# Attention scores as pairs of 64-partition products, with the attention stage ordered by head pairs

## The reference

```
scores = jnp.einsum('bqgnh,bknh->bnqk', gq, k) / jnp.sqrt(jnp.float32(d_head))
scores = jnp.where(causal, IGNORE, scores)
pattern = jax.nn.softmax(scores, axis=-1)
z = jnp.einsum('bknh,bnqk->bqnh', v, pattern)
attn_out = jnp.einsum('bqnh,nhd->bqd', z, W_O)
```

## Time and profile before

| | |
|---|---|
| median of the runs | 610.9 us |
| span of the profiled execution | 607.1 us (its own time is not listed apart from the span) |
| PE busy | 541.2 us, 89% |
| PE weight loads | 425.8 us, 70% |
| DVE / ACT / POOL busy | 387.2 / 305.8 / 182.2 us |
| fills of queries, keys, values | 176.2 to 218.9 us |
| attention, first to last score | 220.2 to 385.85 us |
| rest of attention and routing | to 419.6 us |
| experts | the rest |

### The profile page before, as it was taken

The page is one execution under the profiler, slowest core; times in us unless marked ns, Lnnn a source line. Parts: engine busy times, 40 slices in busy tenths (PEclk is TensorE's granted clock), DMA queues, the critical chain, the costliest instruction groups (busy, mean ns, idle before and its releaser), DMA issues. The chain is left out here.

```text
span 607.1 us, 9890 instructions
## 1 busy us (share of the span) xinstructions
PE 541.2 (89%) x3178; PEld 425.8 (70%) x3179; DVE 387.2 (64%) x972; ACT 305.8 (50%) x552; POOL 182.2 (30%) x269
## 2 busy tenths in 40 slices
PE   1997976999988989999999999954899999999995
PEld 1645864797877866666766766733888888888883
DVE  4986678647375564776865757535666666666661
ACT  1486362215315574555555646413666666666661
POOL 3704449102033123464423231011122222222222
PEclk9999999899999985999999999985999999999999
DMA  8995020000010038000000000991122221222212
GB/s 337 391 335 173 2 70 1 0 1 1 0 36 1 1 123 362 9 28 28 28 1 28 1 27 8 357 354 55 17 37 31 35 37 34 33 34 34 34 18 25
DMA packets 25779, 47.44 MB, mean 78 GB/s; under 512 B 2192, under 2 KB 21136, under 8 KB 25360
## 3 DMA queue, kind: packets, MB, share of 16 engines
q1 hardware_dynamic: 21232, 41.35, 19.0%
q0 software_dynamic: 4080, 5.15, 5.7%
q10 hardware_dynamic: 432, 0.49, 0.3%
HBM read 32.01 MB, written 14.98 MB: 77 GB/s over the span
## 5 line engine op out<-in xcount | busy, mean ns | idle before, releaser
L1596 PE MATMUL ps<-split,xsT 128*128 128x352 f32 x552 | 95.9, 331 | 0.7 <-DVE split L1246 0.7
L1596 PEld LDWEIGHTS ps<-split,xsT 128*128 128x128 f32 x552 | 89.9, 192 | 1.0 <-issue 1.0
L1118 DVE TENSOR_REDUCE nmax<-ps 128x1 f32<-128x128 f32 (+7 forms) x64 | 48.3, 756 | 42.1 <-PE ps L1507 41.2
L1246 DVE TENSOR_TENSOR split<-early,split 128x1408 fp32r<-128x1408 f32 x46 | 72.6, 1618 | 1.9 <-ACT split L784 1.9
L1618 PE MATMUL ps<-mid,work 128*128 (+1 forms) x276 | 67.9, 387 | 0.8 <-ACT work L773 0.8
L784 ACT CAST split<-early 128x1408 fp32r x46 | 62.7, 1366 | 0.9 <-issue 0.9
L1618 PEld LDWEIGHTS ps<-mid,work 128*128 128x128 f32 (+1 forms) x276 | 49.7, 189 | 13.4 <-issue 8.7
L1227 DVE TENSOR_TENSOR work<-work,ps 128x704 f32<-128x704 f32 x23 | 20.4, 888 | 56.8 <-PE ps L1596 56.8
L565 POOL TENSOR_TENSOR rstd<-mhalf 128x1 f32<-128x1 f32 x23 | 11.4, 496 | 138.7 <-ACT work L780 138.7
L1502 PE MATMUL ps<-k_hi,q_split 128*128 128x512 f32 (+3 forms) x96 | 43.8, 456 | 3.2 <-ACT mid L715 1.3
L1504 PE MATMUL ps<-k_lo,q_split 64*128 64x512 f32 (+3 forms) x96 | 44.0, 458 | 0.0
(11 more groups left out here) (249 smaller groups left out, 1160.0 us busy)
## 6 DMA issues: line engine op xcount, KB each, us to landing
early<-m_w SPq DMA_DIRECT2D x16, 704.0 KB, 8.4
expert_in<-pad SPq DMA_DIRECT2D x8, 1040.0 KB, 12.5
mid<-m_w SPq DMA_DIRECT2D x8, 640.0 KB, 10.4
work<-expert_in SPq DMA_DIRECT2D x23, 130.0 KB, 2.5
early<-factors SPq DMA_DIRECT2D x1, 2048.0 KB, 12.4
early<-wq SPq DMA_DIRECT2D x1, 2048.0 KB, 16.8
mid<-f_w SPq DMA_DIRECT2D x1, 2048.0 KB, 21.2
rows<-x_in SPq DMA_DIRECT2D x2, 512.0 KB, 5.3
```

The source lines that it names most:

```text
L1118: V.tensor_reduce(nmax[:, u:u + 1], src, AX_X, ALU.max, negate=True).then_inc(s_max, 1)
L1246: V.tensor_tensor(lo, (ew1, ew3)[w][:, bass.ds(e, 1), :], hi.bitcast(F32), ALU.subtract).then_inc(s_wlo[w], 1)
L1596: last = mm(ps[:, 2 * w + a, 0:IH], xsT[px][b][:, k, :], split_w[w][pw][:, k, a * IH:(a + 1) * IH], start=(k == 0 and px == pw), stop=(k = ...
```

## The change

`k_hi` and the two query parts become 128-partition tensors of four head pairs: a head has one half of the partitions. A key fill is one copy by ScalarE and one subtraction by VectorE. GpSimd makes `q_hi` and `q_lo` by one instruction each per pair. `scores(m)` now does a pair: the two masks first, then three 64-row products per bank (high x high, low x high, high x low), head 0 in rows 0 to 63 and head 1 in rows 64 to 127 in turn. For tiles 0 to 3 a pair has two banks of four, for tiles 4 to 7 all four. The loops of PE, ACT and DVE run over pairs m, with the once-per-tile work at given m % 4. As `k_hi` is half as large, five blocks of w3 load early and three late.

```diff
--- before.py
+++ after.py
@@ -100,8 +100,8 @@
-        K_AT = 2 * E * KD * I - HEADS * T
-        k_hi = view(overlay("k_hi", K_AT, HEADS * T), 0, HEADS, T)
+        K_AT = 2 * E * KD * I - QB * T
+        k_hi = view(overlay("k_hi", K_AT, QB * T), 0, QB, T)
@@ -155,7 +155,7 @@
-        q_split = view(overlay("q_split", 5120, HEADS * P), 0, HEADS, P)
+        q_hi, q_lo = (view(overlay(name, 5120 + i * QB * P, QB * P), 0, QB, P) for i, name in enumerate(("q_hi", "q_lo")))
         work = sb("work", 7 * 1024)
@@ -312,14 +312,21 @@
+        PAIRS = HEADS // 2
+        STEPS = TT * PAIRS
+
         def k_parts(q):
-
             g, j = divmod(q, 12)
             c = slice(g * GW, (g + 1) * GW)
-            for h in range(2):
-                half, other = slice(h * DH, (h + 1) * DH), slice((1 - h) * DH, (2 - h) * DH)
-                n = 2 * (j - 4) + h
-                yield half, k_hi[half, n, c], k_hi[other, n, c], k_lo[half, j - 4, c]
+            return k_hi[:, j - 4, c], k_lo[:, j - 4, c]
+
+        def score_banks(u):
+            m, h = divmod(u, 2)
+            return 2 * h if m // PAIRS >= GT else 2 * (m % 2) + h
+
+        def score_row(u):
+            at = score_banks(u)
+            return ps[:, at:at + 2, :].rearrange("p a b -> p (a b)")[:, 0:(u // HEADS + 1) * P]
@@ -385,8 +392,8 @@
             for e in range(early_w3, E):
-                heads_over = -(-(E * KD * I + (e + 1) * KD * I - K_AT) // T)
-                sp.wait_ge(s_sc, (TT - 1) * HEADS + min(heads_over, HEADS))
+                pairs_over = -(-(E * KD * I + (e + 1) * KD * I - K_AT) // T)
+                sp.wait_ge(s_sc, (TT - 1) * HEADS + 2 * min(pairs_over, PAIRS))
                 sp.dma_start(ew3[:, e], m_w3[:, e]).then_inc(s_e13, 16)
@@ -508,22 +515,14 @@
             def split_queries(m):
-
-
-                i, pair = divmod(m, HEADS // 2)
-                if m >= HEADS // 2:
-                    pool.wait_ge(s_sc, 2 * (m - HEADS // 2) + 2)
-                for h in range(2):
-                    half, other = slice(h * DH, (h + 1) * DH), slice((1 - h) * DH, (2 - h) * DH)
-                    nc.gpsimd.tensor_copy(q_split[half, 2 * pair + h, :],
-                                          qT[half, pair, i * P:(i + 1) * P]).then_inc(s_qhi, 1)
-                pool.wait_ge(s_qhi, 2 * m + 2)
-                for h in range(2):
-                    half, other = slice(h * DH, (h + 1) * DH), slice((1 - h) * DH, (2 - h) * DH)
-                    nc.gpsimd.tensor_tensor(q_split[other, 2 * pair + h, :], qT[half, pair, i * P:(i + 1) * P],
-                                            q_split[half, 2 * pair + h, :].bitcast(F32), ALU.subtract).then_inc(s_qs, 1)
-                    pool.wait_ge(s_qs, 2 * m + h + 1)
-
+                i, pair = divmod(m, PAIRS)
+                if m >= PAIRS:
+                    pool.wait_ge(s_sc, 2 * (m - PAIRS) + 2)
+                q = qT[:, pair, i * P:(i + 1) * P]
+                nc.gpsimd.tensor_copy(q_hi[:, pair, :], q).then_inc(s_qhi, 1)
+                pool.wait_ge(s_qhi, m + 1)
+                nc.gpsimd.tensor_tensor(q_lo[:, pair, :], q, q_hi[:, pair, :].bitcast(F32),
+                                        ALU.subtract).then_inc(s_qs, 1)
@@ -705,10 +704,7 @@
                     act.wait_ge(s_qkv, q + 1)
-                    for half, hi, hi_other, lo in k_parts(q):
-                        nc.scalar.copy(hi, ps[half, 2 + q % 6, :])
-                        last = nc.scalar.copy(hi_other, ps[half, 2 + q % 6, :])
-                    last.then_inc(s_qa, 1)
+                    nc.scalar.copy(k_parts(q)[0], ps[:, 2 + q % 6, :]).then_inc(s_qa, 1)
                 elif q % 2 == 0:
@@ -721,8 +717,7 @@
                     act.wait_ge(s_pt, u - 3)
-                src = ps[:, 2 * (u % 2):2 * (u % 2) + 2, :].rearrange("p a b -> p (a b)")[:, 0:w]
-                nc.scalar.activation(probs[u % 4][:, 0:w], src, ACT.Exp, bias=nmax[:, u:u + 1],
+                nc.scalar.activation(probs[u % 4][:, 0:w], score_row(u), ACT.Exp, bias=nmax[:, u:u + 1],
                                      accum_out=psums[:, u:u + 1]).then_inc(s_pr, 1)
@@ -751,17 +746,21 @@
-            for u in range((TT + 1) * HEADS + 5):
-                if u >= 2 * HEADS and u % HEADS == 0:
-                    routed_feature_major(u // HEADS - 2)
-                if u >= 2 * HEADS and u % HEADS == 2:
-                    logits_exp(u // HEADS - 2)
-                if HEADS <= u < (TT + 1) * HEADS and u % HEADS == 4:
-                    z_feature_major(u // HEADS - 1)
-                if 3 <= u < TT * HEADS + 3:
-                    probs_feature_major(u - 3)
-                if u < TT * HEADS:
-                    attend(u)
+            for m in range(STEPS + 7):
+                i, rel = divmod(m, PAIRS)
+                if rel == 2 and 1 <= i <= TT:
+                    z_feature_major(i - 1)
+                if 1 <= m <= STEPS:
+                    probs_feature_major(2 * m - 2)
+                if rel == 0 and i >= 2:
+                    routed_feature_major(i - 2)
+                if rel == 1 and i >= 2:
+                    logits_exp(i - 2)
+                if m < STEPS:
+                    attend(2 * m)
+                    attend(2 * m + 1)
+                if 1 <= m <= STEPS:
+                    probs_feature_major(2 * m - 1)
@@ -1103,19 +1102,16 @@
                     dve.wait_ge(s_qa, scalar_fills(q))
-                    for half, hi, hi_other, lo in k_parts(q):
-                        last = V.tensor_tensor(lo, ps[half, 2 + q % 6, :], hi.bitcast(F32), ALU.subtract)
-                    last.then_inc(s_qd, 1)
+                    hi, lo = k_parts(q)
+                    V.tensor_tensor(lo, ps[:, 2 + q % 6, :], hi.bitcast(F32), ALU.subtract).then_inc(s_qd, 1)
                 elif q % 2:
                     dve.wait_ge(s_qkv, q + 1)
                     dst, scale = qv_dst(q)
                     V.tensor_scalar(dst, ps[:, 2 + q % 6, :], scale, None, ALU.mult).then_inc(s_qd, 1)
             def row_max(u):
-                w = (u // HEADS + 1) * P
                 dve.wait_ge(s_sc, u + 1)
-                src = ps[:, 2 * (u % 2):2 * (u % 2) + 2, :].rearrange("p a b -> p (a b)")[:, 0:w]
-                V.tensor_reduce(nmax[:, u:u + 1], src, AX_X, ALU.max, negate=True).then_inc(s_max, 1)
+                V.tensor_reduce(nmax[:, u:u + 1], score_row(u), AX_X, ALU.max, negate=True).then_inc(s_max, 1)
@@ -1183,24 +1179,26 @@
             link(V.tensor_scalar(base_e[:, 0, :], iota[:, 0:E], float(T), None, ALU.mult))
-            for u in range((TT + 1) * HEADS + 5):
-                if u < TT * HEADS:
-                    row_max(u)
-                if 1 <= u < TT * HEADS + 1:
-                    normalised(u - 1)
-                if HEADS <= u < (TT + 1) * HEADS and u % HEADS == 5:
-                    add_attention(u // HEADS - 1)
-                    route_variance(u // HEADS - 1)
-                if HEADS <= u < (TT + 1) * HEADS and u % HEADS == 6:
-                    route_normalise(u // HEADS - 1)
-                if u >= 2 * HEADS and u % HEADS == 1:
-                    route_max(u // HEADS - 2)
-                if u >= 2 * HEADS and u % HEADS == 2:
-                    route_choice(u // HEADS - 2)
-                if u >= 2 * HEADS and u % HEADS == 3:
-                    route_tail(u // HEADS - 2)
-                if u >= 2 * HEADS and u % HEADS == 4:
-                    route_slots(u // HEADS - 2)
+            for m in range(STEPS + 7):
+                i, rel = divmod(m, PAIRS)
+                if rel == 2 and i >= 2:
+                    route_slots(i - 2)
+                if rel == 1 and i >= 2:
+                    route_max(i - 2)
+                if 1 <= m <= STEPS:
+                    normalised(2 * m - 2)
+                    normalised(2 * m - 1)
+                if rel == 3 and 1 <= i <= TT:
+                    add_attention(i - 1)
+                    route_variance(i - 1)
+                if m < STEPS:
+                    row_max(2 * m)
+                    row_max(2 * m + 1)
+                if rel == 3 and 1 <= i <= TT:
+                    route_normalise(i - 1)
+                if rel == 1 and i >= 2:
+                    route_choice(i - 2)
+                    route_tail(i - 2)
@@ -1491,21 +1489,26 @@
-            def scores(u):
-                i, n = divmod(u, HEADS)
-                half = slice(64 * (n % 2), 64 * (n % 2) + 64)
-                if u >= 2:
-                    pe.wait_ge(s_pr, u - 1)
-                pe.wait_ge(s_qs, 2 * (u // 2) + 2)
-                for a in range(i // 4 + 1):
-                    w = min((i + 1) * P - a * 512, 512)
-                    mm(ps[:, 2 * (u % 2) + a, 0:w], q_split[:, n, :], k_hi[:, n, a * 512:a * 512 + w],
-                       start=True, stop=False)
-                    mm(ps[:, 2 * (u % 2) + a, 0:w], q_split[half, n, :], k_lo[half, n // 2, a * 512:a * 512 + w],
-                       start=False, stop=(a < i // 4))
-                c = (i % 4) * P
```

(57 more changed lines are left out.)

## The result

The changed kernel takes 586.65 us (median of four runs, 584.7 to 589.36) against 611.02 for the kernel before: a ratio of 0.9618, 95% interval 0.9582 to 0.9653, or 24 us less. The forecast was 14 less, 597, with a range from 589: right in direction, too small, and the time lies outside the range.

The account below looks back on a forecast made before the run. Attention was taken as bound by TensorE's own stream, with 0.2 us lost per height change. Terms -3.2 - 1.5 - 9.9 + 0.4 = -14.2 on the 607.1 span gave 592.9; plus 3.8, 597 us, range 589 to 607.

Parts of the forecast that it names:

- rival B: Score stream: half-height loads stay in front of their products, a round 0.43; +19, 616 us; chance 0.03.
- two row halves at once: Attention scores: both heads' half-height products stream together, a 512-column round taking 0.24 us, bounds 0.23 and 0.46.
- rival A: Score stream: the two heads take turns, a round 0.46; +20, 617 us, slower; chance 0.07.
- the narrow rounds are held by their loads: Scores, tiles 4 to 6: narrow rounds cost two loads, 2 x 0.11, so a pair's scores stay 2.0 us.
- the extras of 2.2 per tile: Tiles 4 to 7: once-per-tile routed copy 0.37, logits' exponential 0.36 and output projection 1.45 add 2.2 us.
- three of 6.36: Tile 7: each pair's cycle is the chain copy, exponential, exponential, scores, 6.36 us, three times before the last scores.
- some 20 us in all less what other work fills: Tiles 4 to 7: TensorE's wait for ScalarE's exponential becomes its largest there, some 20 us before other work fills it.
- The counts, +0.9: Tile 3: the router's counts wait for a choice behind two maxima on VectorE, +0.9, leaving net -0.5; tiles 2, 1 likewise.
- the 0 of tile 0: Tile 0: no change in length, since a pair's scores of 1.1 us replace 1.0.
- case D: Tile 1: the clock rises earlier, so tile 1 runs at full clock, 4 shorter; 593 us; chance 0.12.
- The fills: K fills before attention: fewer ScalarE casts and VectorE subtractions save 1.5 at the first group and 1.7 at the second.
- the end (+0.4): After the last score: two maxima, two exponentials and then copies in ScalarE's order end some 0.4 us later.

Follow-up runs that it names:

- New: The changed kernel itself, with the whole change against the kernel before: 586.65 us, ratio 0.9618.
- an edit of one line: Kernel before, with the product of K's low part taking all 128 rows instead of 64 (scores not the reference's): 582.21 us, ratio 0.9553.
- the 578 us version: Kernel before with K's low-part product at 128 rows, plus ScalarE's second copies of K given to GpSimd: 578.02 us, ratio 0.9502.
- the one re-ordering tried: New products, fills and query split in the old loops over heads, with ScalarE's copy placed behind the exponential: 634.96 us, ratio 1.0414.

## Why the prediction came out too small

**Right: what bounded the kernel.** TensorE's stream, and in it the 0.2 lost at each change between 128 and 64 rows. The page TensorEngine Tiling (Array Packing) of the Trainium skill, section Key Properties, has a drain at a change of mode. Taking the changes out between a head's score products is worth 27 us in the order of before (24 at like clock, 20 in tiles 2 to 7 alone) and 30 in the new. The Trainium skill's rule of row groups (TensorE: Matmul & The Clock Gate, Part 3), rival B's, is not borne out: products of one row group follow each other at 0.23, at full height in a score stream as in the earlier trace rows, and at half height in the run with both heads in one half.

**Right: two row halves at once.** Held between 0.23 and 0.46 for lack of a row, taken as 0.24, measured 0.23 per round. With both heads in one half the round is 0.46, as rival A had it; what that costs it had too low, 20 for 25 at like clock.

**Wrong: "the narrow rounds are held by their loads".** The term 2 x 0.11 put the loads of two heads one behind the other; the rounds of 128 columns take 0.11 in all. Scores of a pair are 0.70 for 1.1 in tile 0 and 1.46 for 2.0 in tile 4 (-2.2 over four pairs, of which the granted clock, 0.92 in that tile against 1.00 before, took up to 1.7). In tile 5 (512 and 256 columns) a part is 0.35 (311.20 to 311.55) for 0.48: -1.6 over four pairs, near the 1.7 found beyond the forecast. In tile 6 (512 and 384) it is 0.41 (327.81 to 328.22): -0.8 of the 1.4.

**Wrong: the extras of 2.2 per tile.** The steps of tile 7 start at 339.72, 345.98, 352.43 and 359.81: 6.26, 6.45 and 7.38 against three of 6.36, 1.0 more in all. The forecast had 1.8 (2.2 of once-per-tile work, less 0.4 for the first step) and 0.4 of hand-offs on top. The projection was charged 1.45 on top of a cycle taken as bound by the chain of copies and exponentials. The cycle's length was right, but its reason was not: at 345.98 TensorE had waited 0.31, and the step that follows is its own stream: scores 1.80, transposes 1.02, values 1.68, transposes 1.31 with the wait of 0.22, counts 0.64. That is 5.6 without wait and counts (the forecast had 5.9, with 32 products of the values for 28), and the once-per-tile work beside it. That work fills the slack between stream and chain before it lengthens anything. It fits this that the waits for exponentials are 2.9 us, where "some 20 us in all less what other work fills" were named, and that single banks in tiles 0 to 3 cost only 2 to 4 where 6 to 14 were expected.

**Wrong: tiles 0 and 1.** "The counts, +0.9" and the 0 of tile 0. In tile 1 both kernels run mostly at the low clock (0.59 against 0.60), and there the rows price the scores: before, a pair's two heads take 1.10 and 1.08 (229.82 to 230.92, 231.00 to 232.08), in New a pair takes 1.29 (224.38 to 225.67). That is 0.9 less for each of the three pairs that run at the low clock in both, 2.7 of the 3.2 found. The forecast had taken that saving from tile 3, at full clock, less 0.9 for the counts. In tile 0 the shorter scores (0.4 per pair below the forecast's 1.1) and the clock (0.85 against 0.64, up to 2.3) would each explain most of the -2.1; they are not separated. The low clock lasted from about 222 to 236 us in New, from 223 to 243 before, so a part of case D (an earlier rise) came true, for a reason that stays open. The clock then took up to 3.5 back in tiles 2 and 4, which no case had; that the two cancel is luck.

**Right, with their runs.** The fills (3.4 against 3.2; undone +4), GpSimd (0), the early w3 (0), the end (+0.4). Of the terms missed all large ones have one sign: 2.1 and 2.7 in tiles 0 and 1, 0.4, 1.7, 1.4 and 1.3 in tiles 4 to 7, together 9.6 of the 10. Tile 2 alone is 0.2 short of its forecast (-0.3 for -0.5), with a clock of 0.89 where it was 1.00.

**What the sum could not see.** The change bought with half-height pairs what an edit of one line gives, within what the clock leaves to be told. The forecast named the waste and then priced only the change's way out of it. Why pairs wait so much in the order of before (28 us, against 8 for the same list of the 578 us version) is not settled: both exponentials of a pair become due together and all four banks come free together, but one bank set alone cost 2 to 4 in the new order, and the one re-ordering tried made it worse.

| us | order of before | order by pairs |
|---|---|---|
| heights mixed (before's products) | 611.0 | 620.4 |
| half height, two heads at once | 604.3 | 586.65 (New) |
| full height, before's fills | 582.2 | 590.6 |
| full height, short fills | 578.0 | 581.6 (not the reference's scores) |

The mean granted clocks of these runs lie between 0.940 and 0.972, so differences of a few us in the table, such as 582.2 against 586.65, are not to be read as the kernels'.

## What to carry to other kernels

In a TensorE stream, take the distance between starts. Here 0.43 where a like product takes 0.23 was a load in the open, and the first thing to try is to make every product the same height, even with rows that add next to nothing, before rebuilding anything. An order written by hand fits one grain of work; changing the grain (one head, two heads) needs the order with it: here the new products alone gave 6 of the 24, and the new order alone nothing. Compare runs of like granted clock before calling a few us a gain. When a forecast adds once-per-tile work to a cycle, check which of two nearly equal chains it falls into.
